# Context attention: in every step the queries' scores are issued first, then the keys' scores and the values

## The reference

```
wq = (q @ wq_w.T + wq_b).reshape(b, t, H, DH)
wk = (k @ wk_w.T + wk_b).reshape(b, t, H, DH)
wv = (v @ wv_w.T + wv_b).reshape(b, t, H, DH)
scores = jnp.einsum('bthd,bshd->bhts', wq, wk) / jnp.sqrt(jnp.float32(DH))
probs = jax.nn.softmax(scores, axis=-1)
attn = jnp.einsum('bhts,bshd->bthd', probs, wv)
attn = attn.reshape(b, t, d)
return attn @ wo_w.T + wo_b
```

## Time and profile before

| | us |
|---|---|
| time, median of 3 runs | 3092.56 |
| lowest, highest | 3082.69, 3092.64 |
| the profiled execution: its own time | 3089.96 |
| the profiled execution: its span | 3088.2 |
| first q of the context attention to its last output projection | 718.89 to 1340.47 |

### The profile page before, as it was taken

One profiled execution on the slowest core, in us unless ns is written; L12 is line 12 of the kernel. 1 busy time (PEld: TensorE's weight loads), 2 busy tenths in 40 slices (PEclk: granted clock), 3 DMA queues, 4 the chain that ended last, 5 costly groups with the idle time before them and its releaser, 6 DMA issues. The chain is left out here.

```text
span 3088.2 us, 31620 instructions
## 1 busy us (share of the span) xinstructions
PE 2559.2 (83%) x11456; PEld 1500.5 (49%) x11456; DVE 1638.7 (53%) x3416; ACT 1385.4 (45%) x1989; POOL 319.5 (10%) x299
## 2 busy tenths in 40 slices
PE   5888888857888888879998588887588888887998
PEld 3555655543333333355455355555344444444555
DVE  5665555525566666615443487878455555541222
ACT  2333333313555555532221565654277777772221
POOL 0110010000000000000166100000121111000000
PEclk8999888867999999978799799998789999998999
DMA  2000000005333333240035411111300000001000
GB/s 71 14 14 14 14 8 14 7 26 143 54 61 61 61 62 56 46 148 1 26 65 78 132 66 45 69 55 42 100 7 28 28 28 28 21 14 62 14 21 21
DMA packets 113394, 140.81 MB, mean 46 GB/s; under 512 B 22004, under 2 KB 96004, under 8 KB 113240
## 3 DMA queue, kind: packets, MB, share of 16 engines
q1 hardware_dynamic: 98888, 123.97, 14.8%
q0 software_dynamic: 11904, 14.69, 2.9%
q10 hardware_dynamic: 2448, 0.14, 0.1%
HBM read 77.89 MB, written 35.39 MB: 37 GB/s over the span
## 5 line engine op out<-in xcount | busy, mean ns | idle before, releaser
L950 DVE TENSOR_REDUCE xattn_tops<-region 128x2 f32<-128x1024 f32 x256 | 305.6, 1219 | 148.2 <-PE region L734 148.1
L887 ACT ACTIVATE xattn_probs<-region 128x1024 f32<-128x1024 f32 x256 | 256.2, 1022 | 154.1 <-PE region L723 153.2
L2085 PE MATMUL region<-psi_fT 128*128 128x512 f32 x512 | 247.3, 622 | 24.7 <-DVE psi_low L2361 15.2
L122 PE MATMUL region<-gla_xT,weights_even 128*128 128x512 f32 (+1 forms) x416 | 207.6, 652 | 31.3 <-ACT gla_xT L214 31.3
L723 PE MATMUL region<-xattn_qs,xattn_ks 49*128 49x512 f32 x512 | 126.6, 496 | 85.0 <-DVE xattn_tops L950 54.5
L122 PE MATMUL region<-mamba_xT,weights_odd 128*128 128x512 f32 x320 | 158.5, 644 | 3.2 <-DVE mamba_xh L1924 3.2
L2085 PEld LDWEIGHTS region<-psi_fT 128*128 128x128 f32 x512 | 93.8, 196 | 135.2 <-issue 101.9
L122 PEld LDWEIGHTS region<-gla_xT,weights_even 128*128 128x128 f32 (+1 forms) x416 | 78.0, 196 | 146.4 <-issue 110.7
L752 PE MATMUL region<-xattn_probs,xattn_va 128*32 128x512 f32 x1024 | 144.7, 633 | 1.3 <-ACT xattn_o_T L914 1.3
L131 PE MATMUL region<-weights_even,gla_work 128*128 128x256 f32 x512 | 123.5, 403 | 26.0 <-ACT gla_work L484 24.7
L734 PE MATMUL region<-xattn_ks,xattn_qs 48*128 48x512 f32 x512 | 126.5, 492 | 14.1 <-DMA xattn_ks<-xattn_khi 9.8
(11 more groups left out here) (501 smaller groups left out, 5226.2 us busy)
## 6 DMA issues: line engine op xcount, KB each, us to landing
weights_even<-mamba_cs SPq DMA_DIRECT2D x32, 512.0 KB, 4.6
xattn_qs<-xattn_qhi SPq DMA_DIRECT2D x128, 64.0 KB, 2.3
xattn_ks<-xattn_khi SPq DMA_DIRECT2D x128, 64.0 KB, 2.3
moe_sums<-moe_picked SPq DMA_DIRECT2D x9, 512.0 KB, 8.7
gla_x<-in_x SPq DMA_DIRECT2D x8, 512.0 KB, 3.8
x_after_gla<-gla_res SPq DMA_DIRECT2D x8, 512.0 KB, 2.9
xattn_x<-x_after_gla SPq DMA_DIRECT2D x8, 512.0 KB, 4.1
xattn_ctxT<-in_ctxT SPq DMA_DIRECT2D x8, 512.0 KB, 4.4
```

Of the source, the lines that this page charges most:

```text
L122: last = st.nc.tensor.matmul(o[0:m, i, :], w[:, c, col + i * P:col + i * P + m], rhs[:, c, :], start=c == 0, stop=c == kc - 1)
L887: A_(probs[:, p % 3, a, :, :], st.region(f"k{v}")[:], ACT.Exp).then_inc(st.emptying(f"k{v}"), 1)
L950: V.tensor_reduce(tops[:, n % 2, t, a::2], st.region(f"q{u}")[:], AX, ALU.max).then_inc(st.emptying(f"q{u}"), 1)
L2085: last = mm(o[:, a, :], fT[:, h, 0, t * P:t * P + P], fT[:, h, 1 + a, :], start=True, stop=True)
```

## The change

In each step of TensorE's loop `by_queries(u)` moves ahead of `by_keys(v)` and `values`. Nothing is added or removed, and the lists of the other engines stay as they are.

```diff
                     if v == 0:
                         pe.wait_ge(st.sem("ones_in"), 32)
+                    if 0 <= u < LAST:
+                        by_queries(u)
                     if 0 <= v < LAST:
                         by_keys(v)
                     if v >= 3 and v % 2 and (v - 3) // 2 < NT * QUADS:
                         values((v - 3) // 2)
-                    if 0 <= u < LAST:
-                        by_queries(u)
                     if u % STEPS == 1 and STEPS < u <= LAST + 1:
                         top_rows(u // STEPS - 1)
```

## The result

The changed kernel takes 3157.35 us (median), the kernel before 3092.6: a ratio of 1.0214, 95% interval 1.019 to 1.0238. One of its four executions took 10490.57 us and was a slow one; it counts in the median but not in the ratio, and the other three took 3154.06 to 3159.5. The profiled execution of after took 3159.5 us. The direction was forecast, the size was not: +66 by the ratio against +44.6, and 3157 lies outside the range of 3108 to 3151.

A forecast was written before the change was run, and what follows sets the result against it. It took the loop k, V, q, maximum between TensorE and VectorE, 3.25 us per pair, as the bound. Its terms, 8.5 + 13.4 + 5.0 + 5.0 + 14.1 - 4.0 + 1.4 + 1.2, summed to 44.6 us: 3134 us, range 3108 to 3151.

The forecast's parts named there:

- The loop and its rotation unchanged: Plain pairs of steps: the loop k, V, q, maximum keeps its order and its 3.25 us, so 0 added.
- T, +0.53: Pairs with `top_rows`: it moves between V and q, onto the loop, +0.53 us each, 16 plain ones, 8.5 us.
- O, +0.84: Pairs with `out_tokens`: moved onto the loop, with VectorE's division waiting for it, +0.84 us each, 16 plain ones, 13.4 us.
- Keys' and queries' projections, +1.6 with the transposed attention: Per batch, 7 times: keys' projection +0.71 us, queries' projection +0.71, transposed attention 0.2; 5.0, 5.0 and 1.4 us.
- Output projection, +2.02: Behind its normalisation the long wait moves one k earlier, so V and O follow it: +2.02 us, 7 times, 14.1.
- the transposed x: Its transposes run under the maximum instead of waiting for one: -0.66 us, 6 times, -4.0 us.
- the sum's silent term for TensorE's clock: TensorE's lower clock behind waits: no term in the 44.6 us sum, only an allowance in the upper bound.
- the upper bound: 3151 us: V and O at the lower clock behind the 3.54 us wait, up to 11, neighbouring pairs some 6.
- slower still: Rival, 3155 us, chance 0.07: waits grow, TensorE's clock falls in one more pair in three quads, 20 us more.
- No change: Rival, 3090 us, chance 0.07: the loop stays at 3.25 us and T and O find cover.
- faster: Rival, about 3065 us, chance 0.05: q issued first behind a projection gives VectorE its next maximum sooner.
- the 3.78 us pair: The pair of steps with T, forecast at 3.78 us instead of 3.25; staying at 3.25 would mean no change.

The follow-up runs named there:

- two densely filled kernels: The changed kernel and the kernel before, each with added 128-row matmuls filling the long TensorE waits: 3092.61 us (ratio 1.003) and 3055.89 us (ratio 0.9899).
- t_ahead: The kernel before with only T (`top_rows`) moved from behind q to between V and q: ratio 0.9986.
- o_ahead: The kernel before with only O (`out_tokens`) moved from behind q to between V and q: 3103.71 us against 3081.63, ratio 1.004.
- div_late: The changed kernel with VectorE's division moved one step later in its list, TensorE's list unchanged: 3134.21 us, ratio 1.016.
- after_dense: The changed kernel with 5, 2, 1, 1 and 12 added 128-row matmuls in steps 18, 21, 22, 23 and 27: 3092.61 us, ratio 1.003.

## Why the prediction was right in direction and wrong in size

The two densely filled kernels separate the terms. At nearly full clock the layers take 637.98 and 597.82 us: the new order costs 40.2 by itself, against a forecast of 44.6. The clock's part is what filling takes off: 690.40 - 637.98 = 52.4 in after, 621.58 - 597.82 = 23.8 in before. The change added 28.6 of it, and 40.2 + 28.6 = 68.8, the whole difference (by construction, as the clock's part is the remainder). This rests on one profiled execution of each kernel, and the batches differ. In the second one the quad with the keys' and queries' projections took 29.16 us in before, not 25.0, and 26.73 in after, not 29.87. In the fifth batch alone the clock's share of the difference is (29.86 - 25.31) - (25.02 - 23.84) + (29.95 - 25.90) - (26.44 - 24.54) = 5.5 us, seven times which would be 39, so 28.6 is good to some 10 us.

- *The loop and its rotation unchanged: right.* Plain pairs are 3.25 us in both.
- *T, +0.53, and O, +0.84: right*, at 0.53 and 0.85 in the plain quads. Alone they cost 0.54 and 0.59, and the later division showed the other 0.25 of O.
- *Keys' and queries' projections, +1.6 with the transposed attention: right at full clock*, 25.31 - 23.84 = 1.5. The odd k behind klo came 9.40 us after its predecessor, 1079.22 to 1088.62, as forecast.
- *Output projection, +2.02: too much at full clock*, 25.90 - 24.54 = 1.4. For the transposed x I had -0.66; the quad shows 14.61 - 14.07 - 1.38 = -0.84.
- *The step that failed is the sum's silent term for TensorE's clock.* I put it at 0, with up to 11 + 6 us in the upper bound; the only reason given is the one against "slower still", that a whole plain quad ran at 1.00 and that no plain wait gets longer. It was 28.6. What stood in the bound came true: V and O behind the long wait take 1.93 and 1.12 us instead of 1.07 and 0.66. Two things were missed, both in the quad with the keys' and queries' projections, whose cost had no term for the clock even in the bound. The queries' projection of after falls into the low stretch, 5.68 us instead of 3.70 in the earlier trace rows, and 5.62 to 5.85 in the last five batches. And behind it, after short waits (1.14, 0.63 and 0.39 us), comes a second low stretch, with V at 1.93. The trace of before had shown at 1057.71 that V can run low in this quad; I had read only the k of 0.80 us, and costed the waits that the change creates by their length.
- *The rivals.* "Slower still (3155)" named the clock and came within 3 us of the result; 0.07 was too little for it. That it came so near is in part luck: it put the loss at 20 us, into one more pair in three quads, where the runs show 28.6 around the projections, and the forecast under it was 4.4 too high. My argument against it, the clock of 1.00 in plain quads, was true and beside the point, as it is not the plain quads that lost. "No change" and "faster" fell with the 3.78 us pair.

On the clock the Trainium skill (TensorE: Matmul & The Clock Gate, A second HAM failure mode: psum-queue depth-cycling) says of one measured kernel that short idle times between groups of matmuls, from cycling through PSUM, came often enough to make the clock swing. This case agrees in part: waits of 0.85 us in every pair left it at 1.00 in the plain quads of before and after, and it fell behind waits around the projections. The Trainium skill (Perfetto Trace Analysis, Matmul Optimizations) also says that the matmul engine scales its power with its utilization, so that matmuls should be issued back to back in batches. The filled kernels agree, with the layer at 0.97 and 0.98 instead of 0.87 and 0.91.

Open: what exactly decides whether a given wait lowers the clock. In t_ahead V behind the same 2.13 us wait kept 1.06 us, and in o_ahead and div_late it alternated from batch to batch, 1.06 or 1.93. Nor is a wait around a projection needed: once in after_dense, behind a wait of 1.10 us in a quad with the transposed x, V took 1.74.

## What to carry to other kernels

Write down the rotation of an issue order before judging a swap: here the swap of q with k and V changed nothing in it, and what really moved was everything pinned to the end of the step, out of the time in which VectorE reads a maximum and onto the loop. Where TensorE's clock falls within a kernel, a change of order has two prices, the one on the chain and the one of the clock around the waits that it makes or lengthens; here the second was 28.6 us against 40.2, and is told apart by filling the waits with matmuls that nobody waits for. Such filling can also be a gain by itself: 1.0% here, and 1.45% together with V ahead of k.

## What was unexpected in the hardware

Added work made a kernel 1.8% faster: a ratio of 1.003 to the kernel before instead of 1.0214, with the layer's granted clock at 0.97 instead of 0.87. And one wait of one length had both outcomes: behind 2.13 us for klo, V took 1.81 to 1.94 us in five of the seven batches of before, and 1.06 or 1.07 in six of t_ahead's (1.10 in the first), with T's place as the only difference.
